# Prologue of a one-core AdaLN, state-space and FFN kernel: POOL's low parts, the modulation and the x projection in another order

## The chip, the cores and the metric

The kernel runs on one core of one Trainium2 chip. The metric is the device time of one execution in microseconds (us); the times of a kernel are the median of its runs. The engines are named as the profile names them: PE (TensorE), DVE (VectorE), ACT (ScalarE), POOL (GpSimd) and SP (SyncE, whose queue issues every DMA of this kernel).

## The reference, cut to what matters

The input u has 4 batches of 512 tokens with 256 channels. A small matrix product of the conditioning c gives six rows of modulation per batch.

```python
mod = (_silu(c) @ wmod).reshape(4, 6, 1, -1)
sa, ca, ga, sb, cb, gb = (mod[:, i] for i in range(6))
...
h = _layernorm(x, axis=-1) * (1 + ca) + sa
x = x + ga * _L0_attn_ref(h, W_in, conv_w, conv_b, z_bias, D, W_out)
h = _layernorm(x, axis=-1) * (1 + cb) + sb
x = x + gb * _L0_ffn_ref(h, W1, W2, W3)
```

In the attention part h is projected by W_in to x (256 channels), B and C (2048 each), z and one a per head (32). x, B and C go through a causal convolution with 4 taps. a goes through a softplus and a running sum over the tokens, and every head's 512 x 512 scores C B^T are weighted by exponents of differences of these sums.

## The kernel before

Everything is float32. A product that must be exact enough is split: each operand has a high part (a cast to the matmul's format) and a low part (the operand minus its high part), and three matmuls hi x hi, hi x lo and lo x hi are added in PSUM.

The order of the work on each engine is written out by hand, as a list of calls in one block per engine, and semaphores tie the engines together. The program has a **prologue** (batch norms, projection and convolution of x, a's running sums), then a long loop over 8 groups of heads times 4 batches (`step`), then the FFN. The change touches the prologue alone. Its chain for a batch b is:

- DVE: `statistics1(b)` (mean and variance of 4 tiles of 128 tokens), POOL: `inverse_root` (1/sqrt of 4 variances for each partition), DVE: `normalise1(b)` (4 instructions that write xn, semaphore `xn_done`).
- PE: `norm_transposes(b)` turns xn into channel rows in PSUM. DVE's `modulation(0)` copies shift and 1 + scale out of PSUM (`mod_ev`); ACT's `h_full(b, kt)` applies them (h32), for both halves kt of the channels. ACT's `h_high` casts h32 to `ht_hi`; POOL's `h_low` subtracts to `ht_lo`.
- PE: `x_project(b, xt)` multiplies by the split weights wx (6 matmuls for each half xt); `a_project(b0)` multiplies h32 of two batches by wa. `warm(n)` issues n matmuls on zeros whose result nobody reads.
- ACT: `x_tap(b, xt)` is the first tap of x's convolution, DVE: `x_tap(b, xt, k)` the three others, each over 512 tokens. With 4 batches and 2 halves DVE has 24 of them.
- a: ACT takes abs, exp and ln, DVE adds (`sp_a`, L1167) and scans over the tokens (L1171, `sums_done`). SP then stores these sums, loads them back broadcast (8 DMAs of `load_sum`), and issues, behind them in its queue, the exchange of x's halves (`swap_halves`) and the stores of x of the batches 2 and 3 (`store_x`). ACT's `last_tap(0, 1, 1)` overwrites the buffer that these stores read and waits for them; `x_evacuate(2, 1)` is queued behind it, and PE's `x_transposes(3, 1)` waits for that.

POOL also splits the weights of x (wx), of the first group of heads (four tiles, `split_tile`) and of z (wz).

The lines that follow are of the kernel before.

Of the kernel before, what the change touches and what calls it, by code (L numbers as in the profile page):

```python
# [19 lines left out]
B, L, D = 4, 512, 256  # L20
# [3 lines left out]
KT = D // P  # L24
CH = L // P
# [3 lines left out]
GT = 4  # L29
# [23 lines left out]
def adaln_ssm_ffn_kernel(nc, u, w_bc, w_x, w_a, w_z, conv, d_rows, z_bias, w_out, w13, w2, c_t, wmod,  # L53
                         consts, out, e_d, gates_d):
    with ExitStack() as ctx:
# [6 lines left out]
        ps = ctx.enter_context(nc.psum_tensor("ps", [P, 8, BANK], F32))  # L62
# [80 lines left out]
        xt = sb("xt", [P, KT, L], F32)  # L143
# [235 lines left out]
        def _(pe):  # L379
# [22 lines left out]
            def norm_transposes(b):  # L402

                pe.wait_ge(s["xn_done"], CH * (b + 1))
                if b >= 2:
                    pe.wait_ge(s["h32_done"], KT * (2 * b - 3))
                for c in range(CH):
                    for kt in range(KT):
                        i = nc.tensor.transpose(ps[:, (4 if b == 1 else 2) + kt, c * P:(c + 1) * P],
                                                xn[:, b % 2, c, kt * P:(kt + 1) * P], ident)  # L410
                i.then_inc(s["lnT_mm"], 1)
# [11 lines left out]
            def x_project(b, xt):  # L423

                pe.wait_ge(s["hlo_done"], KT * (b + 1))
                if b >= 2:
                    pe.wait_ge(s[f"xtaps{xt}"], 3 * (b - 1))
                for kt in range(KT):
                    i = split_mm(ps[:, GT * (b % 2) + xt, :], wx_hi[:, xt, kt, :], wx_lo[:, xt, kt, :],
                                 ht_hi[:, kt, b * L:(b + 1) * L], ht_lo[:, kt, b * L:(b + 1) * L],  # L430
                                 kt == 0, kt == KT - 1)
                i.then_inc(s["xp_mm"], 1)

            def a_project(b0):

                pe.wait_ge(s["h32_done"], KT * (b0 + 2))
                for kt in range(KT):
                    for b in (b0, b0 + 1):
                        i = mm(ps[b * NH:(b + 1) * NH, 6, :], wa_sb[:, kt, :], h32[:, b % 2, kt, :],
                               start=(kt == 0), stop=(kt == KT - 1), skip_group_check=True)  # L440
                        if kt == KT - 1:
                            i.then_inc(s["a_mm"], 1)
# [35 lines left out]
            def warm(n):  # L478

                for k in range(n):  # L480
                    mm(ps[:, 1, :], zeros[:, 0:P], zeros[:], start=True, stop=True)  # L481
# [20 lines left out]
            modulation((0, 1), 0)  # L502
            pe.wait_ge(s["ld_ident"], 16)
            norm_transposes(0)
            norm_transposes(1)
            warm(10)
            pe.wait_ge(s["ld_wa"], 16)
            a_project(0)
            norm_transposes(2)
            pe.wait_ge(s["mod_ev"], 2)  # L510
            pe.wait_ge(s["wx_split"], 2)
            x_project(0, 0)
            x_project(0, 1)
            norm_transposes(3)
            x_project(1, 0)
            x_project(1, 1)
            a_project(2)
            x_project(2, 0)
            pe.wait_ge(s["ld_wmod2"], 16)
# [260 lines left out]
        def _(act):  # L780
# [5 lines left out]
            def h_full(b, kt):  # L786

                n = KT * b + kt
                act.wait_ge(s["lnT_mm"], b + 1)
                if b >= 2:  # L790
                    act.wait_ge(s["hlo_done"], n - 3)
                    act.wait_ge(s["a_mm"], 2)
                af(h32[:, b % 2, kt, :], ps[:, (4 if b == 1 else 2) + kt, :], ACT.Identity, bias=shift[:, 0, kt, b:b + 1],
                   scale=scale1[:, 0, kt, b:b + 1]).then_inc(s["h32_done"], 1)

            def h_high(b, kt):

                act.wait_ge(s["h32_done"], KT * b + kt + 1)
                nc.scalar.copy(ht_hi[:, kt, b * L:(b + 1) * L], h32[:, b % 2, kt, :]).then_inc(s["hhi_done"], 1)

            def x_tap(b, xt):

                n = 2 * b + xt
                act.wait_ge(s["xp_mm"], n + 1)
                w = conv_sb[:, NG * GT + xt, :]
                af(acc[:, n // GT, n % GT, :], ps[:, GT * (b % 2) + xt, :], ACT.Identity, bias=w[:, TAPS:TAPS + 1],
                   scale=w[:, TAPS - 1:TAPS]).then_inc(s["xtap"], 1)
# [7 lines left out]

            act.wait_ge(s["mod_ev"], 2)
            h_full(0, 0)
            h_full(0, 1)
            h_full(1, 0)
            h_high(0, 0)  # L820
            h_full(1, 1)
            h_high(0, 1)
            h_high(1, 0)
            h_high(1, 1)
            h_full(2, 0)
            h_high(2, 0)
            h_full(2, 1)
            act.wait_ge(s["ld_conv"], 16)
            x_tap(0, 0)
            h_high(2, 1)  # L830
            x_tap(0, 1)
            h_full(3, 0)
            h_full(3, 1)
            x_tap(1, 0)
# [234 lines left out]
        def _(dve):  # L1069
# [40 lines left out]
            def normalise1(b):  # L1110
                if b >= 2:
                    dve.wait_ge(s["lnT_mm"], b - 1)
                normalise(u_sb[:, b * CH:(b + 1) * CH, :], xn[:, b % 2], b, norm1_names)
# [12 lines left out]
            def modulation(n):  # L1126

                dve.wait_ge(s["mod_mm"], 4 * (n + 1))
                mod = ps[:, 7 * n, 0:2 * KT * B].rearrange("p (k m b) -> p k m b", k=2, m=KT)
                nc.vector.tensor_copy(shift[:, n], mod[:, 0]).then_inc(s["mod_ev"], 1)  # L1130
                ts(scale1[:, n], mod[:, 1], 1.0, None, ALU.add).then_inc(s["mod_ev"], 1)
# [10 lines left out]
            statistics1(0)  # L1142
            statistics1(1)
            normalise1(0)
            normalise1(1)
            modulation(0)
            statistics1(2)
            statistics1(3)
            normalise1(2)
# [247 lines left out]
        def _(pool):  # L1397
# [37 lines left out]
            def inverse_root(n, eps_name, name):  # L1435

                await_unit(eps_name, n + 1)
                gp.tensor_tensor(rstd[:, n % 2], vareps[:, n % 2], minus_half[:], ALU.pow).then_inc(s[name], 1)  # L1438

            def h_low(b, kt):  # L1440

                pool.wait_ge(s["hhi_done"], KT * b + kt + 1)
                gp.tensor_tensor(ht_lo[:, kt, b * L:(b + 1) * L], h32[:, b % 2, kt, :],
                                 ht_hi[:, kt, b * L:(b + 1) * L].bitcast(F32), ALU.subtract).then_inc(s["hlo_done"], 1)
# [4 lines left out]
            gp.tensor_copy(wx_hi[:], wx_raw[:]).then_inc(s["wx_split"], 1)  # L1449
            pool.wait_ge(s["wx_split"], 1)  # L1450
            gp.tensor_tensor(wx_lo[:], wx_raw[:], wx_hi[:].bitcast(F32), ALU.subtract).then_inc(s["wx_split"], 1)
            inverse_root(2, "eps1", "rs")
            inverse_root(3, "eps1", "rs")
            h_low(0, 0)
            h_low(0, 1)
            h_low(1, 0)
            h_low(1, 1)
            h_low(2, 0)
            pool.wait_ge(s["ld_wg"], 16)
            split_tile(0, 1)  # L1460
            h_low(2, 1)
            split_tile(0, 0)
            h_low(3, 0)
            split_tile(0, 3)
            split_tile(0, 2)
            h_low(3, 1)
            pool.wait_ge(s["ld_wz"], 16)
            gp.tensor_copy(wz_hi[:], wz_raw[:]).then_inc(s["wz_split"], 1)
            pool.wait_ge(s["wz_split"], 1)
# [220 lines left out]
```

## Time and profile before

| what | value |
|---|---|
| median of 3 runs | 534.34 us (533.17 to 534.63) |
| profiled execution, its own time | 538.0 us |
| its span in the profile | 535.8 us |
| mean granted clock of PE | 0.987 |
| PE busy | 520.5 us, 97% |
| DVE busy | 451.6 us, 84% |
| ACT busy | 367.1 us, 69% |
| POOL busy | 240.0 us, 45% |

The span is what the profile's times count from; 2.2 us of the profiled execution's own time lie around it. A busy share is an average over the program; the prologue is its first 60 us. In a timeline a row is a run of like instructions: start, time from the first one's start to the last one's end, engine, line, operation, output and inputs, their number, and in brackets the idle time of the engine before it with what ended it. Neighbours on one engine overlap by some 0.1 us in these rows, so a start to the next start is the better measure of what an instruction costs in a row.

### The profile page before, as it was taken

The page shows a single profiled execution, that of the slowest core. Times are in us where ns is not written, and L with a number is a line of the kernel's source. Part 1 is how long each engine was busy: PE and PEld are TensorE (multiplying, and loading weights), DVE is VectorE, ACT ScalarE, POOL GpSimd, SP SyncE. Part 2 cuts the span into 40 slices and gives each one's busy share as a digit, 9 for nine tenths or more (in the row PEclk, how much of TensorE's full clock was granted, in tenths as well). Part 3 has the DMA queues.
Part 4 walks back from the last instruction along what each step waited for, and adds up shares of the span by engine and source line. Part 5 has one row for each costly group of instructions (what it writes and reads, how often), then busy time and mean ns, then how long its engine had stood idle before and what let it go on. Part 6 is the DMA issues. An engine that isn't in the chain of part 4 may idle for free.

```text
span 535.8 us, 19307 instructions
## 1 busy us (share of the span) xinstructions
PE 520.5 (97%) x7188; PEld 429.9 (80%) x7188; DVE 451.6 (84%) x746; ACT 367.1 (69%) x988; POOL 240.0 (45%) x465
## 2 busy tenths in 40 slices
PE   6998999999999999999999999998999999999997
PEld 3666788888888888888888888876889889889886
DVE  6899699999999999999999999998666656656342
ACT  1777789899898998988899899887424224234240
POOL 6763237777776766776786474581000000000000
PEclk9899899999999999999999999999999999999999
DMA  7736153343333335332432535576430232100101
GB/s 248 299 111 214 49 144 102 98 130 112 109 108 102 125 100 180 128 102 84 142 93 84 152 89 163 146 219 193 125 95 25 80 81 77 40 0 2 40 0 40
DMA packets 50289, 59.40 MB, mean 111 GB/s; under 512 B 8004, under 2 KB 44740, under 8 KB 49864
## 3 DMA queue, kind: packets, MB, share of 16 engines
q1 hardware_dynamic: 50248, 58.88, 35.9%
q8 instruction: 22, 0.36, 0.3%
q14 instruction: 19, 0.16, 0.1%
HBM read 48.75 MB, written 9.05 MB: 108 GB/s over the span
## 4 chain that ended last, share of the span: by engine, by line
PE 87%; DVE 4%; DMA 4%; SPq 2%; issue 1%; POOL 1%; ACT 1%; DVEq 0%; ACTq 0%; POOLq 0%
PE ps L384 20%; PE ps L385 20%; PE ps L386 20%; PE ps L574 9%; PE ps L548 5%; PE ps L629 4%; PE ps L595 3%; PE ps L612 3%; PE ps L698 2%; DVE acc L1123 2%; DMA gates<-gate_rows 2%; DMA x_channels<-acc 1%; SPq L247 1%; PE ps L481 1%; DMA u_sb<-in_u 1%
## 5 line engine op out<-in xcount | busy, mean ns | idle before, releaser
L1212 DVE SCALAR_TENSOR_TENSOR acc<-ps,cw_dve,acc 128x511 f32<-128x511 f32 (+2 forms) x384 | 255.9, 738 | 6.2 <-ACT acc L863 5.9
L1512 POOL TENSOR_TENSOR sums<-sums,far_above 128x256 f32<-128x256 f32 x128 | 94.5, 742 | 112.5 <-DMA sums<-packed_sums 106.4
L898 ACT ACTIVATE decay<-sums,p_slot 128x128 f32<-128x128 f32 (+1 forms) x512 | 143.2, 363 | 1.2 <-ACT p_slot L975 0.7
L863 ACT ACTIVATE acc<-ps,cw_act 128x512 f32<-128x512 f32 x128 | 95.4, 769 | 18.7 <-PE ps L386 16.6
L384 PE MATMUL ps<-ht_hi,wg_hi 128*128 128x512 f32 x256 | 107.5, 420 | 0.1
L385 PE MATMUL ps<-ht_lo,wg_hi 128*128 128x512 f32 x256 | 101.9, 398 | 0.0
L386 PE MATMUL ps<-ht_hi,wg_lo 128*128 128x512 f32 x256 | 101.9, 398 | 0.0
L1039 ACT ACTIVATE silu_sb<-ps 128x512 f32<-128x512 f32 x32 | 19.2, 599 | 78.6 <-PE ps L386 78.6
L1438 POOL TENSOR_TENSOR rstd<-vareps,minus_half 128x4 f32<-128x4 f32 x8 | 8.4, 1047 | 121.9 <-DVE vareps L1093 119.6
L386 PEld LDWEIGHTS ps<-ht_hi,wg_lo 128*128 128x128 f32 x256 | 48.5, 189 | 11.6
L1350 DVE TENSOR_TENSOR hid<-ps,silu_sb 128x512 f32<-128x512 f32 x32 | 22.1, 691 | 42.0 <-ACT silu_sb L1039 41.8
L384 PEld LDWEIGHTS ps<-ht_hi,wg_hi 128*128 128x128 f32 x256 | 48.6, 190 | 9.7 <-issue 0.6
L385 PEld LDWEIGHTS ps<-ht_lo,wg_hi 128*128 128x128 f32 x256 | 49.0, 191 | 8.9
L574 PE MATMUL ps<-acc 64*64 64x64 f32 (+1 forms) x2048 | 52.3, 250 | 0.1
L384 PE MATMUL ps<-h_hi,w_hi 128*128 128x512 f32 x128 | 50.5, 394 | 0.0
L574 PEld LDWEIGHTS ps<-acc 64*64 64x64 f32 x2048 | 47.6, 133 | 3.1
L386 PE MATMUL ps<-h_hi,w_lo 128*128 128x512 f32 x128 | 49.9, 390 | 0.0
L385 PE MATMUL ps<-h_lo,w_hi 128*128 128x512 f32 x128 | 49.9, 390 | 0.0
L887 ACT COPY b_tok<-ps 128x384 f32<-128x384 f32 x64 | 30.4, 474 | 14.5 <-PE ps L548 14.1
L1199 DVE TENSOR_TENSOR mix<-ps,decay 128x1024 f32<-128x1024 f32 x32 | 38.8, 1213 | 0.0
L384 PE MATMUL ps<-w_hi,hid_hi 128*128 128x256 f32 x128 | 37.0, 289 | 0.2 <-DVE stage L1366 0.2
L385 PE MATMUL ps<-w_lo,hid_hi 128*128 128x256 f32 x128 | 36.2, 283 | 0.0
(144 smaller groups left out, 917.6 us busy)
## 6 DMA issues: line engine op xcount, KB each, us to landing
sums<-packed_sums SPq DMA_DIRECT2D x256, 96.0 KB, 2.7
wg_raw<-in_w_bc SPq DMA_DIRECT2D x8, 512.0 KB
y_parts<-yt_sb SPq DMA_DIRECT2D x64, 64.0 KB, 2.1
stage<-y_parts SPq DMA_DIRECT2D x32, 128.0 KB, 2.9
u_sb<-in_u SPq DMA_DIRECT2D x4, 512.0 KB, 4.9
stage<-in_w SPq DMA_DIRECT2D x1, 2048.0 KB, 14.0
x_channels<-acc SPq DMA_DIRECT2D x8, 256.0 KB, 2.5
ee<-running_sums SPq DMA_DIRECT2D x8, 256.0 KB, 3.9
```

Source lines behind the costliest of these rows:

```text
L384: mm(o, w_hi, x_hi, start=first, stop=False)
L385: mm(o, w_hi, x_lo, start=False, stop=False)
L386: return mm(o, w_lo, x_hi, start=False, stop=last)
L548: i = nc.tensor.transpose(ps[:, 6 if p else PROJ_BANK[0], c * P:(c + 1) * P], acc[:, b % 2, p, c * P:(c + 1) * P], ident)
L574: i = mm(ps[NS * at:NS * (at + 1), SCORE_BANKS[bank], o:o + P - NS * h], acc[own, b % 2, p, c * P + NS * h:c * P + NS * (h + 1)], acc[own, ...
L863: af(acc[:, b % 2, t, :], ps[:, PROJ_BANK[t], :], ACT.Identity, bias=cw_act[:, t, 1:2], scale=cw_act[:, t, 0:1]).then_inc(s[f"tap_a{t}"], 1)
L887: nc.scalar.copy(b_tok[:, p, :], ps[:, 6 if p else PROJ_BANK[0], 0:3 * P]).then_inc(s["bt_ev"], 1)
L898: i = af(decay_f[:, m:m + P - NS * h], sums[:, j, own], ACT.Exp, scale=-1.0, bias=p_slot[:, b * CH + n, j:j + 1])
L1199: tt(mix_f[:, 0:2 * BANK].rearrange("p (a l) -> p a l", a=2), ps[:, 2:4, :], decay_f[:, 0:2 * BANK].rearrange("p (a l) -> p a l", a=2), AL ...
L1212: stt(a[:, d:], ps[:, PROJ_BANK[t], 0:L - d], cw_dve[:, t, TAPS - 1 - d:TAPS - d], a[:, d:], ALU.mult, ALU.add).then_inc(s[f"taps{t}"], 1)
L1350: tt(hid[:, m % 2, :], ps[:, 2 + m % 2, :], silu_sb[:, m % 2, :], ALU.mult).then_inc(s["hid_done"], 1)
L1512: gp.tensor_tensor(v, v, far, ALU.add).then_inc(s["masked"], 1)
```

## The change

It does five things, all in the prologue.

1. POOL computes the low parts of batch 0 ahead of the inverse roots of the batches 2 and 3, then waits until DVE has written all norms (`xn_done` at 16), then computes the other six low parts, and only then splits the four weight tiles, which stood between them.
2. DVE's `modulation(0)` stands between the norms of batch 0 and of batch 1.
3. PE has 5 warming matmuls in place of 10, ahead of the transposes of batch 1.
4. PE projects x of the batches 0 and 1 in two parts: the 8 matmuls on the high part of h, for which the low part isn't needed, then the 4 on its low part. Batch 0 stands ahead of `a_project(0)`; batch 1's transposes of batch 3 stand between its parts.
5. ACT casts batch 0 as soon as each half is there, and does batch 0's two taps ahead of batch 2.

```diff
+            def x_project_high(b):
+                pe.wait_ge(s["hhi_done"], KT * (b + 1))
+                for xt in range(2):
+                    for kt in range(KT):
+                        o, x = ps[:, GT * (b % 2) + xt, :], ht_hi[:, kt, b * L:(b + 1) * L]
+                        mm(o, wx_hi[:, xt, kt, :], x, start=(kt == 0), stop=False, skip_group_check=True)
+                        mm(o, wx_lo[:, xt, kt, :], x, start=False, stop=False, skip_group_check=True)
+            def x_project_low(b):
+                pe.wait_ge(s["hlo_done"], KT * (b + 1))
+                for xt in range(2):
+                    for kt in range(KT):
+                        i = mm(ps[:, GT * (b % 2) + xt, :], wx_hi[:, xt, kt, :], ht_lo[:, kt, b * L:(b + 1) * L],
+                               start=False, stop=(kt == KT - 1), skip_group_check=True)
+                    i.then_inc(s["xp_mm"], 1)
...
             norm_transposes(0)
+            pe.wait_ge(s["mod_ev"], 2)
+            warm(5)
             norm_transposes(1)
-            warm(10)
+            pe.wait_ge(s["wx_split"], 2)
+            x_project_high(0)
+            x_project_low(0)
             pe.wait_ge(s["ld_wa"], 16)
             a_project(0)
             norm_transposes(2)
-            pe.wait_ge(s["mod_ev"], 2)
-            pe.wait_ge(s["wx_split"], 2)
-            x_project(0, 0)
-            x_project(0, 1)
+            x_project_high(1)
             norm_transposes(3)
-            x_project(1, 0)
-            x_project(1, 1)
+            x_project_low(1)
             a_project(2)
...
             act.wait_ge(s["mod_ev"], 2)
             h_full(0, 0)
+            h_high(0, 0)
             h_full(0, 1)
+            h_high(0, 1)
             h_full(1, 0)
-            h_high(0, 0)
             h_full(1, 1)
-            h_high(0, 1)
             h_high(1, 0)
             h_high(1, 1)
-            h_full(2, 0)
-            h_high(2, 0)
-            h_full(2, 1)
             act.wait_ge(s["ld_conv"], 16)
             x_tap(0, 0)
+            x_tap(0, 1)
+            h_full(2, 0)
+            h_full(2, 1)
+            h_high(2, 0)
             h_high(2, 1)
-            x_tap(0, 1)
             h_full(3, 0)
...
             normalise1(0)
+            modulation(0)
             normalise1(1)
-            modulation(0)
...
+            h_low(0, 0)
+            h_low(0, 1)
             inverse_root(2, "eps1", "rs")
             inverse_root(3, "eps1", "rs")
-            h_low(0, 0)
-            h_low(0, 1)
+            pool.wait_ge(s["xn_done"], CH * B)
             h_low(1, 0)
             h_low(1, 1)
             h_low(2, 0)
+            h_low(2, 1)
+            h_low(3, 0)
+            h_low(3, 1)
             pool.wait_ge(s["ld_wg"], 16)
             split_tile(0, 1)
-            h_low(2, 1)
             split_tile(0, 0)
-            h_low(3, 0)
             split_tile(0, 3)
             split_tile(0, 2)
-            h_low(3, 1)
```

On PE, at the start of the program, the order of before is this (L481 is `warm`, L397 the modulation's product, L409 a batch's 8 transposes as one or two batches in a row, L439 `a_project`, L384 to L386 one split product of x):

```order
L481 MATMUL ps<-sums 128x512 x20
L397 MATMUL ps<-c_silu,wmod_sb 32x4 x32
L409 MATMUL ps<-cst,xn 128x128 x16
L481 MATMUL ps<-sums 128x512 x10
L439 MATMUL ps<-h,wa_sb 32x512 x4
L409 MATMUL ps<-cst,xn 128x128 x8
L384 MATMUL ps<-ht_hi,wx_hi 128x512
L385 MATMUL ps<-ht_lo,wx_hi 128x512
L386 MATMUL ps<-ht_hi,wx_lo 128x512
```

The same stretch of the changed kernel (L499 is `warm`, L440 and L441 the high part's matmuls, of which three more pairs follow ahead of L448, the low part's; L457 is `a_project`):

```order
L499 MATMUL ps<-sums 128x512 x20
L397 MATMUL ps<-c_silu,wmod_sb 32x4 x32
L409 MATMUL ps<-cst,xn 128x128 x8
L499 MATMUL ps<-sums 128x512 x5
L409 MATMUL ps<-cst,xn 128x128 x8
L440 MATMUL ps<-ht_hi,wx_hi 128x512
L441 MATMUL ps<-ht_hi,wx_lo 128x512
...
L448 MATMUL ps<-ht_lo,wx_hi 128x512 x4
L457 MATMUL ps<-h,wa_sb 32x512 x4
L409 MATMUL ps<-cst,xn 128x128 x8
```

So x of batch 0 has moved ahead of `a_project(0)` and of batch 2's transposes, and half of the warming matmuls are gone.

On POOL, in the middle of the prologue, the order of before is this (rstd is an inverse root, ht_lo a low part of h, wg the split of a weight tile, wz that of z's weights):

```order
L1451 TENSOR_TENSOR wx_lo<-wx_raw,wx_hi 128x512
L1438 TENSOR_TENSOR rstd<-vareps,minus_half 128x4 x2
L1443 TENSOR_TENSOR ht_lo<-h,ht_hi 128x512 x5
L1431 CAST wg_hi<-wg_raw 128x256
L1433 TENSOR_TENSOR wg_lo<-wg_raw,wg_hi 128x256
L1443 TENSOR_TENSOR ht_lo<-h,ht_hi 128x512
L1431 CAST wg_hi<-wg_raw 128x256
L1433 TENSOR_TENSOR wg_lo<-wg_raw,wg_hi 128x256
L1443 TENSOR_TENSOR ht_lo<-h,ht_hi 128x512
```

The same stretch of the changed kernel:

```order
L1469 TENSOR_TENSOR wx_lo<-wx_raw,wx_hi 128x512
L1461 TENSOR_TENSOR ht_lo<-h,ht_hi 128x512 x2
L1456 TENSOR_TENSOR rstd<-vareps,minus_half 128x4 x2
L1461 TENSOR_TENSOR ht_lo<-h,ht_hi 128x512 x6
L1449 CAST wg_hi<-wg_raw 128x256
L1451 TENSOR_TENSOR wg_lo<-wg_raw,wg_hi 128x256
L1449 CAST wg_hi<-wg_raw 128x256
L1451 TENSOR_TENSOR wg_lo<-wg_raw,wg_hi 128x256
```

Two low parts have moved ahead of the last two inverse roots; the six others stand together behind them, and behind the wait for the norms; all four weight splits follow. SP's order is the same in both kernels.

## Rows read from the trace of the kernel before

**Rows 1.** The page: the span, and each engine's busy time.

```profile
span 535.8 us, 19307 instructions
PE 520.5 (97%) x7188; PEld 429.9 (80%) x7188; DVE 451.6 (84%) x746; ACT 367.1 (69%) x988; POOL 240.0 (45%) x465
```

**Rows 2.** Windows of PE: length, busy (count), granted clock, DMA share, GB/s.

```profile
15.00:16.00 1.00, 1.00 (x4) 0.50 1.00 406
...
57.00:58.00 1.00, 1.00 (x4) 0.50 0.00 0
```

**Rows 3.** The chain of work that ended last, from 30 to 56 us.

```profile
35.45 1.14 DVE sums_t L1171
...
47.90 5.28 DMA x_channels<-acc
```

**Rows 4.** Timeline of DVE in the prologue.

```profile
13.09 1.39 DVE L1087 BATCH_NORM_STATS2 stats<-u_sb 128x6 f32<-128x256 f32 x4
...
16.83 1.38 DVE L1100 TENSOR_SCALAR xn<-u_sb,meanvar,rstd 128x256 f32<-128x256 f32 x4
18.36 5.02 DVE L1100 TENSOR_SCALAR xn<-u_sb,meanvar,rstd 128x256 f32<-128x256 f32 x4 [0.15 <-POOL rstd L1438]
24.72 0.75 DVE L1123 SCALAR_TENSOR_TENSOR acc<-ps,conv_sb,acc 128x511 f32<-128x511 f32 x1 [1.34 <-ACT acc L806]
25.83 8.88 DVE L1123 SCALAR_TENSOR_TENSOR acc<-ps,conv_sb,acc 128x511 f32<-128x511 f32 x13 [0.36 <-ACT acc L806]
...
35.37 1.21 DVE L1171 TENSOR_TENSOR_SCAN sums_t<-reset,sp_a 128x512 f32<-128x512 f32 x1
```

**Rows 5.** Timeline of POOL in the prologue.

```profile
11.29 1.26 POOL L1451 TENSOR_TENSOR wx_lo<-wx_raw,wx_hi 128x512 fp32r<-128x512 f32 x1
...
17.09 1.16 POOL L1438 TENSOR_TENSOR rstd<-vareps,minus_half 128x4 f32<-128x4 f32 x1 [0.89 <-DVE vareps L1093]
18.08 6.54 POOL L1443 TENSOR_TENSOR ht_lo<-h,ht_hi 128x512 fp32r<-128x512 f32 x5
...
25.14 0.73 POOL L1433 TENSOR_TENSOR wg_lo<-wg_raw,wg_hi 128x256 fp32r<-128x256 f32 x1 [0.18 <-POOL wg_hi L1431]
...
35.37 2.28 POOL L1470 TENSOR_TENSOR wz_lo<-wz_raw,wz_hi 128x512 fp32r<-128x512 f32 x1
```

**Rows 6.** Timeline of ACT in the prologue.

```profile
13.20 1.45 ACT L793 ACTIVATE h<-ps,shift,scale 128x512 f32<-128x512 f32 x2 [10.62 <-DVE scale L1131]
...
16.94 1.65 ACT L799 CAST ht_hi<-h 128x512 fp32r<-128x512 f32 x3
...
25.68 1.45 ACT L793 ACTIVATE h<-ps,shift,scale 128x512 f32<-128x512 f32 x2
...
29.00 1.12 ACT L799 CAST ht_hi<-h 128x512 fp32r<-128x512 f32 x2
...
33.85 0.63 ACT L844 ACTIVATE a_work<-a_work 128x512 f32<-128x512 f32 x1
```

**Rows 7.** Timeline of PE in the prologue.

```profile
10.39 1.06 PE L409 MATMUL ps<-cst,xn 128*128 128x128 f32 x8 [1.20 <-DVE xn L1100]
13.07 1.97 PE L409 MATMUL ps<-cst,xn 128*128 128x128 f32 x8 [1.62 <-DVE xn L1100]
...
18.85 1.91 PE L439 MATMUL ps<-h,wa_sb 128*32 128x512 f32 x8
...
21.54 0.48 PE L384 MATMUL ps<-ht_hi,wx_hi 128*128 128x512 f32 x1
...
24.43 1.04 PE L409 MATMUL ps<-cst,xn 128*128 128x128 f32 x8
...
28.21 1.91 PE L439 MATMUL ps<-h,wa_sb 128*32 128x512 f32 x8
...
54.65 0.63 PE L453 MATMUL ps<-cst,acc 128*128 128x128 f32 x4 [2.29 <-ACT x_tok L813]
...
56.62 0.63 PE L384 MATMUL ps<-ht_hi,wg_hi 128*128 128x512 f32 x1
```

## The prediction, made before the changed kernel ran

> **What bounds the kernel now.** I read the page first: PE is busy for 520.5 of 535.8 us [rows 1], so what happens in the prologue counts only through the moment at which PE can leave it. The reader should therefore look for what PE waits for in the first 55 us. PE's timeline shows it: idle for 2.29 us until 54.65, ended by ACT's copy of x [rows 7]. The chain of waits, followed back from there, says what that copy stood behind [rows 3]: a convolution tap that waited for the stores of x, issued until 47.90 and landed 5.28 later; these came after a row of SP's issues; and the first of those waited for a's running sums, whose scan starts on DVE at 35.45 in the chain and ends at 36.59. From the scan's end to 54.65 are 18.1 us in which SP issues DMAs back to back and waits for transfers. The change touches none of it. So the question is how much earlier the scan ends.
>
> Ahead of the scan DVE is the tight engine. It does 13 taps without a gap from 25.83 to 34.7, then a's sum and the scan [rows 4]: 8.88/13 gives 0.68 a tap where they follow each other. Ahead of that it loses time. The four norms of batch 2 took 1.38 us, the like four of batch 3 took 5.02 [rows 4], in a stretch where POOL did low parts of h, 5 in 6.54 us [rows 5]; then DVE stood 1.34 and 0.36 for taps from ACT [rows 4].
>
> **What the change costs and gives, step by step.** I carry the times of before through the new orders.
>
> *Start.* PE transposes batch 0 at 10.39 to 11.45 [rows 7]. ACT started only at 13.20, since the modulation's copy on DVE stood behind both norms [rows 6]; now the modulation is there by 10.6 (batch 0's norms are done at 10.39 [rows 7], and two copies of 8 columns follow), and ACT starts at 11.5. An h takes 0.78 and the next follows after 0.67; casts in a row follow after 0.51 and take 0.62 [rows 6]. With a cast behind its own h, ACT has both halves of batch 0 cast at 11.5 + 2 x (0.78 + 0.62) less a 0.1 of overlap, 14.2. POOL's two low parts (6.54/5, 1.3 each [rows 5]) end at 15.5; before, they ended at 18.08 + 2.6, 20.7.
>
> *PE to its next fixed point.* The modulation wait costs nothing (10.6 against 11.45). The 5 warming matmuls run at 11.45; those of before took (18.85 - 15.04)/10, 0.4 each, since PE's granted clock was 0.50, its lower level of 1.2 GHz [rows 2, 7]. So they end at 13.3. The transposes of batch 1 take 1.97 at that level and end near 15.2 [rows 7]; x's weights are split by 12.55 [rows 5]. A matmul of x at 2.4 GHz costs (24.43 - 21.54)/12, 0.24 [rows 7]. Then high part 8 x 0.24 to 17.1; low part 4 x 0.24 to 18.05 (its input is there at 15.5); `a_project(0)` 1.85 to 19.9; transposes of batch 2 to 20.95; high part of batch 1 to 22.85; transposes of batch 3 to 23.9; low part to 24.85. The transposes of batch 3 also need ACT to have emptied the banks of batch 2: 20.95 + 1.5, in time.
>
> *The norms.* Statistics of the batches 2 and 3 take 13.09 to 16.83 as before [rows 4]. The inverse roots (1.1 each [rows 5]) stand behind the low parts, 15.5, and are there at 16.6 and 17.7. The first is still ahead of the end of the statistics, 16.8, so batch 2's norms come as before, by 18.2; a root beside them does not hold them (1.38 with the root at 17.09 beside them [rows 4, 5]). Batch 3's take 1.4 instead of 5.0 because POOL stands still: done by 19.3, 4 us earlier. PE wants them at 22.85. POOL then does batch 1's low parts 19.3 to 21.9, and PE wants them at 23.9: 2 us of slack, which is the price of POOL's wait, fully covered. Whether statistics are themselves held by a low part no row shows. Bounds: nothing, or, held as the norms were, up to two low parts, 2.6 us, which pushes the last norm to 21.9 at most and batch 1's low parts to 24.5; then PE stands 0.6. I take nothing, as the low end of 0 to 0.6.
>
> *ACT and DVE after it.* ACT does batch 3's two h from 23.9 to 25.4 and the taps of batch 1 at 25.25, so DVE's sixth tap can start at 26.0. Before it started at 25.83 + 4 x 0.68, 28.5 [rows 4]. `a_project(2)` starts at 25.4, 2.8 earlier than 28.21 [rows 7]. DVE is no longer late for itself here: it has done its first five taps by 19.3 + 5 x 0.68, 22.7, and waits 3.3. From the sixth tap on DVE, PE and ACT keep their order. ACT's last casts go from 29.00 to 26.5, and with it the end of the ln from 34.48 to about 32.0 [rows 6]; DVE, which wanted it 0.7 ahead of the scan at 35.37, wants it at 34.7 - 2.6, 32.1. So the three engines move together by 2.5 to 2.8. I take 2.6.
>
> *The scan.* POOL's weight splits, which stood between low parts, come later: the last low part starts after ACT's casts and ends at 29.8, and the four subtractions of 0.73 [rows 5] fall, one every 1.3 us, between 30.3 and 34.8. The scan falls between 32.7 and 33.9, so it meets one. Before it met the split of z: the subtraction took 2.28, where the same shape took 1.26 [rows 5], and the scan its full speed of 1.21 [rows 4]. So it was POOL that waited there, 1.0. Here it can be either: if it is the scan, that costs up to the 0.7 of a subtraction, if it is POOL, nothing. I take 0.2, nearer to the row, in which the scan ran and POOL waited. The Trainium skill has this as a rule (SBUF — State Buffer, Who interferes with whom): a VectorE instruction with two SBUF inputs and a GpSimd instruction that reads SBUF exclude each other, and whichever starts first holds the port for its whole length. By that rule, the trace of before agrees (2.28 against 1.26), and a subtraction that starts ahead of the scan would charge up to 0.7, which gives 1.9 and 532.4. The weight tiles are wanted by PE at 37.4, so their delay costs nothing.
>
> *Behind the scan* the 18.1 us stay, as SP's order is the same and the loads at the start have long landed. PE arrives at its wait 2.4 earlier too, so the idle 2.29 remains, and the stretch at the lower level that follows it, with matmuls 0.43 apart instead of 0.24 [rows 2, 7] (the row at 56.62 is one of eight), remains.
>
> Sum: 2.6 - 0.2 = **2.4 us less**. The profiled execution would go from 538.0 (span 535.8) to 535.6 (span 533.4). The median of the runs shown is 3.7 lower than that execution; the same step from 534.34 gives **531.9 us**, 0.45% faster.
>
> **Rivals.**
>
> *The clock stays low a stretch longer.* PE has less to do ahead of x now, 5 warming matmuls less. Before, it stood idle from 11.45 to 13.07, was at the lower level at 15 to 16 and back at the higher by 18.85 [rows 2, 7]. If it stays low from 15.2 to about 18.6, x of batch 0 costs 0.43 a matmul, 1.5 us more, all of it on PE's way to 24.85. Then 0.9 us less than before, 533.4. For it: nothing shows what PE needs to be raised. Against: in the new order PE works without a gap from 10.39 on. I give 0.17.
>
> *The clock comes back sooner or the second fall is missed.* The first saves 0.9 on batch 1's transposes, the second eight matmuls by 0.19, 1.5. Then 3.3 to 3.9 less: 530.4 to 531.0. Chance 0.12.
>
> *The gain is lost on the way to 54.65.* The stores of x landed in 5.28 us beside other transfers; if they collide otherwise, or the scan waits its 0.7 and ACT's ln is later than I add up, 0.3 to 1.2 us are left: 533.1 to 534.0. Chance 0.14. Against: every transfer there is issued in the same order at the same distance.
>
> *It ends on the other side.* The place is PE from 15.2 on; the mechanism is again the lower level, as long as in the first stretch of before, which lasted from the idle at 11.45 to at most 18.85, 7 us. A low stretch of 7 us from 15.2 costs 7 x (1 - 0.24/0.43), 3.1 us, 0.7 more than the gain: 535.0. It decides from 5.4 us of lower level on; 9 us would be slower by 1.6. For it: x_project's high part would then be the first dense work. Against: before, ten dense matmuls at the lower level were enough to end it. Chance 0.07.
>
> That the edit does not do what it says (DVE's norms still held because POOL's inverse roots hold them) has the rows against it that I gave: 1.38 beside a root.
>
> **How the numbers follow.** The forecast itself, 1.8 to 2.9 less, has 0.50. The likeliest time is 531.9, its own range 531.4 to 532.6. A change below 0.3%, 1.6 us, cannot be told from none here. Faster by more: 0.50 + 0.12, and 0.03 of the third rival's upper end, 0.65. Within: 0.29. Slower by more: 0.06, most of the fourth. For 8 in 10 the range takes in the missed fall of the clock (530.4) and the first and third rival down to 534.0; it leaves out the slower one.
>
> **What would show it.** Right: norms of batch 3 in 1.4 us; ACT's first h near 11.5; DVE's first tap before 20 with a new idle of about 3 us behind the fifth; the scan's end at 34 to 34.4; PE's idle ending near 52.2. Wrong: a granted clock of 0.50 beyond 16 us, the scan stretched to 1.9, low parts of batch 1 that PE waits for, or an idle ahead of 52 us that grew by as much as the prologue gained.

## The result and the profile after

The changed kernel took 531.25 us in the median of 7 runs (529.46 to 531.95), the kernel before 534.63 us in 7 runs beside them (533.17 to 536.10). The ratio is 0.9921 with a 95% interval of 0.9894 to 0.9949, so 0.8% faster, 3.4 us where 2.4 were forecast. Run again later, it gave 531.20 us in 12 runs (529.94 to 534.25), ratio 0.9951, interval 0.9928 to 0.9974. Over all the runs whose clock is listed, which the 7 of the kernel before above are not, the medians are 534.37 us (94 runs of the kernel before) and 531.21 us (19 of the changed one), 3.2 us apart. The first set's 531.25 us lies just below the prediction's own range (531.4 to 532.6) and inside its range for 8 in 10 (530.4 to 534.0).

The two profiled spans differ by far more, 535.8 [rows 1] against 527.6:

```profile
span 527.6 us, 19297 instructions
PE 513.4 (97%) x7182; PEld 425.6 (81%) x7183; DVE 446.5 (85%) x746; ACT 367.2 (70%) x988; POOL 239.8 (45%) x465
```

That is one execution of each, and part of the 8.2 us is chance. At the end of PE's wait near 50 us the two are 5.3 us apart: 3.8 at the scan's end and 1.5 more behind it. The other 2.9 come later, where PE's granted clock fell to 0.50 twice more in the kernel before (56 to 59 us and 374 to 376 us) and not once in this execution of the changed kernel. First DVE's timeline of the changed kernel, which answers to [rows 4]:

```profile
12.49 1.41 DVE L1105 BATCH_NORM_STATS2 stats<-u_sb 128x6 f32<-128x256 f32 x4 [1.14 <-DMA u_sb<-in_u]
...
16.74 2.68 DVE L1118 TENSOR_SCALAR xn<-u_sb,meanvar,rstd 128x256 f32<-128x256 f32 x8 [0.16 <-POOL rstd L1456]
19.33 3.63 DVE L1141 SCALAR_TENSOR_TENSOR acc<-ps,conv_sb,acc 128x511 f32<-128x511 f32 x5
24.94 6.00 DVE L1141 SCALAR_TENSOR_TENSOR acc<-ps,conv_sb,acc 128x511 f32<-128x511 f32 x9 [1.99 <-ACT acc L824]
...
31.60 1.22 DVE L1189 TENSOR_TENSOR_SCAN sums_t<-reset,sp_a 128x512 f32<-128x512 f32 x1
```

The norms of the batches 2 and 3 are one run of 8 in 2.68 us, where the last four alone had taken 5.02. The first tap starts at 19.33 instead of 24.72. Then the new idle, 1.99 us ahead of the sixth tap, and the scan's row starts at 31.60 instead of 35.37.

POOL's timeline, which answers to [rows 5]:

```profile
13.14 2.52 POOL L1461 TENSOR_TENSOR ht_lo<-h,ht_hi 128x512 fp32r<-128x512 f32 x2
15.62 2.22 POOL L1456 TENSOR_TENSOR rstd<-vareps,minus_half 128x4 f32<-128x4 f32 x2
19.50 5.11 POOL L1461 TENSOR_TENSOR ht_lo<-h,ht_hi 128x512 fp32r<-128x512 f32 x4 [1.66 <-DVE xn L1118]
26.16 2.55 POOL L1461 TENSOR_TENSOR ht_lo<-h,ht_hi 128x512 fp32r<-128x512 f32 x2 [1.55 <-ACT ht_hi L817]
...
31.76 1.59 POOL L1451 TENSOR_TENSOR wg_lo<-wg_raw,wg_hi 128x256 fp32r<-128x256 f32 x1 [0.18 <-POOL wg_hi L1449]
```

POOL stands still for 1.66 us until the norms are done, and the subtraction of the third weight split, which starts 0.16 us after the scan, waits for it: 1.59 us where it takes 0.73 alone [rows 5].

ACT and PE, which answer to [rows 6, 7]:

```profile
11.21 0.78 ACT L811 ACTIVATE h<-ps,shift,scale 128x512 f32<-128x512 f32 x1 [8.47 <-PE ps L409]
```

```profile
12.02 1.04 PE L409 MATMUL ps<-cst,xn 128*128 128x128 f32 x8
14.12 0.47 PE L440 MATMUL ps<-ht_hi,wx_hi 128*128 128x512 f32 x1 [1.05 <-ACT ht_hi L817]
...
16.06 1.09 PE L448 MATMUL ps<-ht_lo,wx_hi 128*128 128x512 f32 x4
17.08 1.91 PE L457 MATMUL ps<-h,wa_sb 128*32 128x512 f32 x8
...
24.29 1.91 PE L457 MATMUL ps<-h,wa_sb 128*32 128x512 f32 x8 [0.60 <-ACT h L811]
...
32.96 1.09 PE L482 MATMUL ps<-cst,sums_t 128*64 128x128 f32 x16 [0.71 <-DVE sums_t L1189]
...
49.33 0.63 PE L471 MATMUL ps<-cst,acc 128*128 128x128 f32 x4 [0.75 <-ACT x_tok L831]
```

The transposes of batch 1 take 1.04 here, not 1.97, because PE's clock did not fall. Windows of PE (length, busy, granted clock, DMA) show it, in answer to [rows 2]:

```profile
12.00:13.00 1.00, 1.00 (x9) 1.00 0.97 352
...
15.00:16.00 1.00, 1.00 (x6) 1.00 1.02 414
```

PE's wait that ended at 54.65 now ends at 49.33, and is 0.75 us instead of 2.29. The row at 32.96 matters below: PE itself waits for the scan, whose sums it transposes.

### The profile page after: what moved, and what is told of

It reads as the page before. It is cut to its first block, busy times and chain, and to the rows that moved or that the text cites. A ratio compares the mean times of both kernels' runs of the same rounds, so it can differ in the third digit from the quotient of the medians.

```text
span 527.6 us, 19297 instructions
## 1 busy us (share of the span) xinstructions
PE 513.4 (97%) x7182; PEld 425.6 (81%) x7183; DVE 446.5 (85%) x746; ACT 367.2 (70%) x988; POOL 239.8 (45%) x465
## 4 chain that ended last, share of the span: by engine, by line
PE 82%; DVE 10%; ACT 2%; DMA 2%; issue 2%; POOL 1%; SPq 0%; DVEq 0%; POOLq 0%; ACTq 0%
PE ps L384 19%; PE ps L385 18%; PE ps L386 18%; PE ps L592 8%; DVE acc L1230 5%; PE ps L566 4%; PE ps L647 4%; PE ps L613 3%; PE ps L630 2%; PE ps L716 2%; DMA gates<-gate_rows 1%; DVE mix L1217 1%; DVE acc L1141 1%; DMA u_sb<-in_u 1%; DVE mix L1219 1%
## 5 line engine op out<-in xcount | busy, mean ns | idle before, releaser
L384 PE MATMUL ps<-ht_hi,wg_hi 128*128 128x512 f32 x256 | 107.0, 418 | 0.0
L386 PE MATMUL ps<-ht_hi,wg_lo 128*128 128x512 f32 x256 | 101.2, 396 | 0.0
L386 PEld LDWEIGHTS ps<-ht_hi,wg_lo 128*128 128x128 f32 x256 | 48.2, 188 | 11.6
L384 PEld LDWEIGHTS ps<-ht_hi,wg_hi 128*128 128x128 f32 x256 | 48.2, 188 | 9.3 <-issue 0.4
L385 PEld LDWEIGHTS ps<-ht_lo,wg_hi 128*128 128x128 f32 x256 | 48.6, 190 | 8.8
L384 PE MATMUL ps<-h_hi,w_hi 128*128 128x512 f32 x128 | 50.5, 394 | 0.0
L386 PE MATMUL ps<-h_hi,w_lo 128*128 128x512 f32 x128 | 49.9, 390 | 0.0
L384 PE MATMUL ps<-w_hi,hid_hi 128*128 128x256 f32 x128 | 37.0, 289 | 0.2 <-DVE stage L1384 0.2
```

The source lines that it names most:

```text
L384: mm(o, w_hi, x_hi, start=first, stop=False)
L385: mm(o, w_hi, x_lo, start=False, stop=False)
L386: return mm(o, w_lo, x_hi, start=False, stop=last)
```

## The experiments

Each was timed against the kernel before on the same chip, and each has one profiled execution. "Like the changed kernel" below means a ratio whose interval overlaps both of the changed kernel's.

### 1. The kernel before, again

> The kernel before, unchanged, to see how its profile and its granted clock differ from one execution to the next. If the 8.2 us between the two profiled spans are all the change, its span is again 535 to 536 with a clock of 0.987 or so. If some of it is chance in PE's clock, its runs spread over several us and the shorter ones have the higher mean clock, by about 1.6 us for each stretch of 3.4 us at the lower level; the chain's step from the scan's end to the end of PE's wait near 54 us stays at about 18.

Measured: 535.68 us (532.01 to 537.92, 10 runs), ratio to its other runs 1.0026 (1.0002 to 1.0050); there is no edit, and the interval still leaves out 1, so a difference of 0.3% is not to be read from such an interval. The profiled span is 532.9. DVE, the chain and PE of this execution:

```profile
24.65 0.75 DVE L1123 SCALAR_TENSOR_TENSOR acc<-ps,conv_sb,acc 128x511 f32<-128x511 f32 x1 [1.75 <-ACT acc L806]
...
35.30 1.21 DVE L1171 TENSOR_TENSOR_SCAN sums_t<-reset,sp_a 128x512 f32<-128x512 f32 x1
```

```profile
47.83 3.89 DMA x_channels<-acc
```

```profile
53.20 0.63 PE L453 MATMUL ps<-cst,acc 128*128 128x128 f32 x4 [0.92 <-ACT x_tok L813]
```

The prologue is the same to 0.07 us up to the scan. Behind it the stores of x land in 3.89 us, not 5.28 [rows 3], and PE's wait ends 1.45 earlier; no fall of the clock follows it. So from the scan's end to the end of that wait are 16.7 us here (35.38 + 1.14, in the chain, to 53.20), not the 18.1 on which the prediction built. That expectation missed. What differed in the transfer is not shown.

The runs also show the clock's part. Each run has a mean granted clock, and the medians go with it:

| mean clock of the run | kernel before | changed kernel |
|---|---|---|
| 1.000 | 532.79 us (2 runs) | 530.12 us (6 runs) |
| 0.997 | 533.16 us (27) | 531.81 us (5) |
| 0.994 | 533.88 us (14) | 531.78 us (4) |
| 0.990 | 535.00 us (41) | none |
| 0.987 | 537.65 us (4) | none |

(Values of the clock between these have one or two runs each and are left out.) At the same mean clock the two are 1.4 to 2.7 us apart. The rest of the 3.2 goes with the clock, whose mean over the runs is 0.9928 before and 0.9968 after. The table shows that time and clock go together, not which fall costs what. The profiles show where the falls are: both of the kernel before have the granted clock at 0.50 from 12 to 18 us and again near 372 us, after PE has waited 2.3 to 2.5 us for a norm. Both of the changed kernel stay up at either place, though PE waited 2.08 and 2.65 us there. Experiments 2 and 8 (0.997) fell only at the second place, which the change does not touch. No path shown here leads from the change to the second place, so that share of the gap may be chance.

### 2. The change without POOL's standing still

```diff
-            pool.wait_ge(s["xn_done"], CH * B)
```

> The changed kernel without POOL's wait for the norms; everything else as changed. Theory A (POOL's standing still frees DVE's norms, but DVE waits for ACT's tap after its fifth tap anyway): the norms of batch 3 go from 1.4 to about 3 to 4 us beside low parts of batch 1, DVE's idle of 2.0 us before the sixth tap shrinks by as much, and the time stays within 0.5 us. Theory B (the wait carries the gain): about 2 us slower than the changed kernel. Theory C (POOL's wait costs more than it gives, since the low parts of batch 1 come 2 us earlier without it): up to 0.3 us faster.

Measured: 531.21 us (12 runs), ratio 0.9950 (0.9930 to 0.9971), like the changed kernel. DVE and POOL:

```profile
19.01 3.08 DVE L1118 TENSOR_SCALAR xn<-u_sb,meanvar,rstd 128x256 f32<-128x256 f32 x4 [0.15 <-POOL rstd L1456]
22.02 9.52 DVE L1141 SCALAR_TENSOR_TENSOR acc<-ps,conv_sb,acc 128x511 f32<-128x511 f32 x14
```

```profile
18.73 2.56 POOL L1461 TENSOR_TENSOR ht_lo<-h,ht_hi 128x512 fp32r<-128x512 f32 x2
```

The norms of batch 3 are held again, 3.08 us instead of 1.38, and DVE has no idle of note among the 14 taps that follow. Most of the 1.7 us come out of the idle that DVE had anyway; the scan's row starts at 32.20, 0.6 later than in the changed kernel's profile. Theory A fits: POOL's wait for the norms is worth nothing that these runs can tell.

### 3. The change with 10 warming matmuls

```diff
-            warm(5)
+            warm(10)
```

> The changed kernel with 10 warming matmuls in place of 5. Theory A (the gain is PE's shorter way through the prologue): at the higher level of the clock five more cost about 1.1 us on PE, of which 1.05 are idle before x's high part now, so 0 to 0.3 us slower; at the lower level 2.1 us, so about 1 us slower. Theory B (PE's clock is what counts, and more dense work keeps it up): a higher mean clock over the runs and 0.5 us or more faster.

Measured: 531.66 us (7 runs), ratio 0.9948 (0.9930 to 0.9967), like the changed kernel, with a mean clock of 0.997 over its runs as well. In its profiled execution, the slowest of the seven, the matmuls ran at the lower level, and the sixth tap came at 26.85 instead of 24.94:

```profile
11.98 3.39 PE L499 MATMUL ps<-sums 128*128 128x512 bf16 x9 [0.22 <-issue]
15.21 1.04 PE L409 MATMUL ps<-cst,xn 128*128 128x128 f32 x8
```

The mean clock is no higher than the changed kernel's, so theory B falls; what the five matmuls cost is within the interval.

### 4. The change with a later scan

```diff
+            for k in range(3):
+                nc.vector.memset(xn2[:], 0.0).then_inc(s["pad"], 1)
+                dve.wait_ge(s["pad"], k + 1)
             dve.wait_ge(s["aln_done"], 1)
```

> The changed kernel with three fills of 1024 columns of an idle buffer on DVE just ahead of the sum of a, which make the scan later by their length (1.5 to 3 us by the row). Theory A (the scan's end sets the end, one to one, through SP's row of issues): the kernel is slower by 0.8 to 1.0 of the scan's delay. Theory B (behind the scan something else decides, as the landing of the stores of x or PE's own work): slower by less than half of the delay.

Measured: 537.21 us (6 runs), ratio 1.0060 (1.0040 to 1.0080). DVE and PE:

```profile
32.19 0.91 DVE L1185 MEMSET xn<- 128x1024 f32 x1 [0.16 <-issue]
...
36.27 1.52 DVE L1192 TENSOR_TENSOR_SCAN sums_t<-reset,sp_a 128x512 f32<-128x512 f32 x1
```

```profile
37.94 1.85 PE L482 MATMUL ps<-cst,sums_t 128*64 128x128 f32 x16 [4.60 <-DVE sums_t L1192]
```

The fills delay the sum of a by 3.6 us (three, each 1.19 after the last), and the median is 6.0 above the changed kernel's 531.21. So the scan's end does set the end, but at more than one to one, which neither theory had. The delay becomes idle time of PE, 4.60 us, and PE works at the lower level after it: the transposes behind it take 1.85, not 1.09, and from the scan's end to the end of PE's wait are 18.1 us, where the changed kernel has 16.5. With the scan, which took 1.52 instead of 1.22, that makes 5.5 of the 6.0.

### 5. POOL's new order alone

On the kernel before, the hunk of POOL from the change, nothing else.

> The kernel before with POOL's new order alone (batch 0's low parts ahead of the last two inverse roots, the wait for the norms, splits last). In the kernel before ACT casts batch 0 only by 17.6 us, so the roots wait behind low parts that end near 19. Theory A (the parts of the change need each other): the norms of batch 3 take 1.4 us but end near 22.6 instead of 23.4, DVE's first tap is not earlier than 24, and the time is within 1 us of before, rather slower. Theory B (POOL's wait alone carries the gain, by freeing DVE's norms of 3.6 us): 2 us or more faster than before.

Measured: 536.23 us (12 runs, one of them 571.0, which the ratio leaves out), ratio 1.0022 (0.9997 to 1.0047): no gain. Theory A fits, B falls. DVE and POOL:

```profile
19.77 2.67 DVE L1100 TENSOR_SCALAR xn<-u_sb,meanvar,rstd 128x256 f32<-128x256 f32 x8 [2.28 <-POOL rstd L1438]
25.24 0.75 DVE L1123 SCALAR_TENSOR_TENSOR acc<-ps,conv_sb,acc 128x511 f32<-128x511 f32 x1 [2.79 <-ACT acc L806]
...
35.89 1.70 DVE L1171 TENSOR_TENSOR_SCAN sums_t<-reset,sp_a 128x512 f32<-128x512 f32 x1
```

```profile
16.20 2.49 POOL L1443 TENSOR_TENSOR ht_lo<-h,ht_hi 128x512 fp32r<-128x512 f32 x2 [4.22 <-ACT ht_hi L799]
```

The norms are freed, and come later: their roots stand behind low parts for which POOL waited 4.22 us, as ACT starts late without the earlier modulation. DVE is done with the norms at 22.4, and then waits 2.79 for the tap.

### 6. Everything but POOL

On the changed kernel, POOL's order of before.

> The changed kernel with POOL's order of before: everything but POOL. Theory A (low parts of batch 0 come behind both roots, from 17.6 on, so PE holds at x's low part of batch 0 until about 20.2 where the changed kernel had it at 16.1): DVE's sixth tap at 28 to 29, scan's end near 36, the time within 1 us of before. Theory B (PE's and ACT's new order with fewer warming matmuls carries the gain): as fast as the changed kernel within 0.7 us.

Measured: 537.82 us (12 runs), ratio 1.0061 (1.0038 to 1.0084), 3.3 us slower than before. PE:

```profile
20.43 1.20 PE L448 MATMUL ps<-ht_lo,wx_hi 128*128 128x512 f32 x4 [3.40 <-POOL ht_lo L1461]
21.56 3.59 PE L457 MATMUL ps<-h,wa_sb 128*32 128x512 f32 x8
```

PE has nothing left ahead of x's low part and waits 3.40 us for POOL; the work behind it runs at the lower level, 3.59 for 1.91. Theory A has the place right and the size too small: the sixth tap comes at 31.11, not at 28 to 29, and the time is not within 1 us of before. Theory B falls.

### 7. The kernel before with 5 warming matmuls

```diff
-            warm(10)
+            warm(5)
```

> The kernel before with 5 warming matmuls in place of 10, nothing else. Theory A (in the kernel before PE reached x of batch 0 at 21.5 where its low part was there at 20.7, so PE's warming was late by at most 0.9 us): 0.5 to 1.0 us faster than before, scan's end 0.8 earlier. Theory B (warming matmuls are the gain): 2 us or more faster. Theory C (less dense work keeps the clock low for longer): slower, with a lower mean clock over its runs.

Measured: 533.27 us (12 runs), ratio 0.9982 (0.9960 to 1.0005). The scan's row starts at 34.87, 0.5 earlier:

```profile
34.87 1.22 DVE L1171 TENSOR_TENSOR_SCAN sums_t<-reset,sp_a 128x512 f32<-128x512 f32 x1
```

Theory A fits, but a ratio of 1 is inside the interval. B and C fall.

### 8. The ln first

```diff
-            x_tap(2, 0)
             act.wait_ge(s["aexp_done"], 1)
             af(a_exp, a_exp, ACT.Ln, bias=1.0).then_inc(s["aln_done"], 1)
+            x_tap(2, 0)
```

and on DVE the taps (2, 0, 0) and (2, 0, 1) behind the scan.

> The changed kernel with ACT's ln (and its table load) ahead of the first tap of batch 2, and DVE's sum and scan of a two taps earlier. The scan's end should come about 1.1 us earlier. Theory A (the scan's end sets the end): about 1 us faster than the changed kernel. Theory B (with the scan at 32.8 PE's own work is as late, as its idle near 49 us is only 0.75): at most 0.7 us faster, the idle near 49 us gone.

Measured: 530.73 us (6 runs), ratio 0.9920 (0.9888 to 0.9952), like the changed kernel. The scan's row starts at 30.38 instead of 31.60. PE no longer waits for the scan, but waits at 36.04 for a tap of DVE that now stands behind the scan; its wait near 49 us ends only 0.55 earlier and is as long as in the changed kernel:

```profile
30.38 1.22 DVE L1187 TENSOR_TENSOR_SCAN sums_t<-reset,sp_a 128x512 f32<-128x512 f32 x1
```

```profile
36.04 0.50 PE L384 MATMUL ps<-ht_hi,wg_hi 128*128 128x512 f32 x1 [0.85 <-DVE acc L1141]
...
48.78 0.63 PE L471 MATMUL ps<-cst,acc 128*128 128x128 f32 x4 [0.75 <-ACT x_tok L831]
```

So 0.7 of 1.2 us are lost behind the scan. B's size fits, but the idle that it wanted gone stayed.

### 9. The kernel before, 5 warming matmuls between the transposes

```diff
+            warm(5)
             norm_transposes(1)
-            warm(10)
```

> The kernel before with 5 warming matmuls, and these between the transposes of batch 0 and batch 1, where the changed kernel has them. The run with 5 in the old place had its lower level of the clock once in the prologue, the kernel before in both its profiles twice in a row. Theory A (the place of the matmuls sets the clock, and the clock alone is not the gain): the lower level lasts at most 3.5 us in the prologue, the scan's end is near 36 as with 5 in the old place, 0.7 to 1.3 us faster than before. Theory B (a clock that stays up is most of the gain): 2 us or more faster than before.

Measured: 534.00 us (12 runs), ratio 0.9988 (0.9968 to 1.0009). The scan's row starts at 34.78, as in experiment 7. The transposes of batch 1 took 1.09, so the clock was up there; it fell later, for `a_project(0)`, 3.05 us instead of 1.91, behind an idle of 2.48:

```profile
16.63 3.05 PE L439 MATMUL ps<-h,wa_sb 128*32 128x512 f32 x8 [2.48 <-ACT h L793]
```

Theory A fits, though a ratio of 1 is inside the interval, and B falls. A clock that is up for the transposes brings nothing that the interval tells to the kernel before, which then waits for ACT's h of batch 1.

### 10. The changed kernel, again

> The changed kernel, unchanged, for its spread and a second profile. If the first profile owed about 1 us to the clock, which stayed up throughout, the runs have scan ends between 32.8 and 34 and spans between 527.6 and 530.5, and most have at least one stretch at the lower level; the median is 530.5 to 531.5.

Measured: as given at the top, 531.20 us. The median is as expected, and 9 of the 12 runs have a mean clock below 1.000; their spans reach 532.4, further than the 530.5 expected. Its profile has a span of 528.5 and again no fall of the clock in the prologue. DVE, and the low parts of POOL beside it:

```profile
14.49 1.25 DVE L1111 TENSOR_SCALAR vareps<-meanvar 128x4 f32<-128x4 f32 x1
...
25.02 6.00 DVE L1141 SCALAR_TENSOR_TENSOR acc<-ps,conv_sb,acc 128x511 f32<-128x511 f32 x9 [1.01 <-ACT acc L824]
...
31.67 1.22 DVE L1189 TENSOR_TENSOR_SCAN sums_t<-reset,sp_a 128x512 f32<-128x512 f32 x1
```

```profile
13.18 2.54 POOL L1461 TENSOR_TENSOR ht_lo<-h,ht_hi 128x512 fp32r<-128x512 f32 x2
```

One thing differs ahead of the sixth tap. The small instruction that adds epsilon to the variances (`vareps`) took 1.25 us where it takes 0.17: it ended with POOL's second low part, which had started at 14.40. In the changed kernel's first profile it ran at 14.26, just ahead of that low part. Here the last norm is done at 20.5, not 19.4, and PE stood 0.30 for batch 1's low part; DVE's idle ahead of the sixth tap took up the rest.

### 11. x of the batches 0 and 1 whole

```diff
-            x_project_high(0)
-            x_project_low(0)
+            x_project(0, 0)
+            x_project(0, 1)
...
-            x_project_high(1)
             norm_transposes(3)
-            x_project_low(1)
+            x_project(1, 0)
+            x_project(1, 1)
```

> The changed kernel with x of the batches 0 and 1 projected whole, three matmuls at a time, which waits for the low parts from the start. In the changed kernel x's high part ran from 14.1 to 16.1 and the low part was there at 15.7. Theory A (high parts first are worth what PE would stand): PE starts x of batch 0 at 15.7 instead of 14.1, 1.5 us later, which passes to the sixth tap and the scan: 1.0 to 1.5 us slower than the changed kernel. Theory B (at the lower level of the clock PE comes at 15.2 anyway): 0.3 to 0.7 us slower.

Measured: 534.31 us (12 runs), ratio 1.0002 (0.9976 to 1.0027): the whole gain is gone. PE:

```profile
16.30 0.47 PE L384 MATMUL ps<-ht_hi,wx_hi 128*128 128x512 f32 x1 [0.81 <-POOL ht_lo L1461]
...
19.26 1.91 PE L457 MATMUL ps<-h,wa_sb 128*32 128x512 f32 x8
21.11 1.09 PE L409 MATMUL ps<-cst,xn 128*128 128x128 f32 x8
23.83 1.07 PE L409 MATMUL ps<-cst,xn 128*128 128x128 f32 x8 [1.63 <-ACT h L811]
...
27.62 1.91 PE L457 MATMUL ps<-h,wa_sb 128*32 128x512 f32 x8
```

Both expectations were too small, since they counted one place of two. The first: PE stands 0.81 for the low part with the high part still to do, and `a_project(0)` starts 2.2 later than at 17.08. Half of that is the clock and the start: experiment 4's profile, whose clock also fell there, has it at 18.16, 1.1 earlier than here. The second: the transposes of batch 3 need the banks that ACT empties of batch 2, and with no high part of batch 1 between the two transposes PE stands 1.63; `a_project(2)` starts 2.2 later than in experiment 4 (27.62 against 25.37). Then the scan met a weight split and, unlike above, was itself held:

```profile
34.70 1.78 DVE L1189 TENSOR_TENSOR_SCAN sums_t<-reset,sp_a 128x512 f32<-128x512 f32 x1
```

### 12. The ln first and ACT's copy ahead of the tap

Experiment 8 and, on ACT:

```diff
             x_evacuate(2, 0)
-            last_tap(0, 1, 1)
             x_evacuate(2, 1)
+            last_tap(0, 1, 1)
```

> The changed kernel with the ln first, as above, and ACT's copy of x that PE waits for near 49 us ahead of the tap that waits for the stores of x. Theory A (PE's own work is the bound there, the copy its last wait of 0.75, and the wait for the stores of x no longer reaches PE): the idle of 0.75 is gone, and the time is 0.5 to 0.9 us below that of the kernel with the ln first, 530.0. Theory B (what PE does next waits for the tap just as long): no change from that kernel, the idle moved to the next transposes.

Measured: 529.63 us (528.80 to 531.57, 8 runs), ratio 0.9915 (0.9886 to 0.9944), the lowest median of the study, 4.7 us below that of the kernel before. The changed kernel's ratio on the same chip was 0.9951 (0.9928 to 0.9974); the intervals overlap, so that it beats the changed kernel is likely and not shown. PE near 49 us:

```profile
47.75 1.04 PE L471 MATMUL ps<-cst,acc 128*128 128x128 f32 x8
48.62 0.49 PE L566 MATMUL ps<-cst,acc 128*128 128x128 f32 x3
49.51 0.48 PE L384 MATMUL ps<-ht_hi,wg_hi 128*128 128x512 f32 x1 [0.40 <-ACT b_tok L905]
```

The two transposes of batch 3 are one run of 8, the wait of 0.75 is gone, and an idle of 0.40 comes back one step on, for another copy of ACT. Theory A holds for the place, and half of the idle has moved as B said. That copy is still queued behind the tap, but the tap waited only 0.15 us here, for PE, and not for the stores of x.

## Why the prediction was right, point by point

- **The start held.** Forecast: ACT's first h at 11.5, casts by 14.2, low parts by 15.5. Measured: 11.21, 13.97, 15.66.
- **The norms held**, in the first profile: all done at 19.4 (19.3), batch 3's in 1.4 us, POOL's wait covered. Statistics beside low parts were not held (1.41 for four in both cases), but the small instruction behind them can be (1.17 to 1.25 for 0.17 in experiments 2, 3, 8, 10, 11 and 12). I had bounded that at 0 to 0.6 us of PE and taken 0; PE stood 0.30 to 0.33 for it in experiments 10 and 12. Experiment 2 goes further than I did: no effect of POOL's wait shows in the time.
- **PE to 24.85 was mis-sized, by the clock.** I placed the high part at 15.2, with 5 matmuls and the transposes at the lower level. In the profiles of experiments 10 and 12 and of the changed kernel the clock stayed up, the high part started at 14.12 to 14.15, held by ACT's cast, and the sixth tap came near 25.0, not 26.0. In experiment 4, whose edit comes later, the clock fell there and the sixth tap came at 26.02, as forecast. So both cases occur. The first set's 3.4 is in the range of the second rival (clock up, 3.3 to 3.9 less), to which I gave 0.12.
- **The scan**: forecast to end near 34.2, it ended at 32.8: 1.1 us from the clock, 0.2 because POOL waited for it (1.59 against 0.73), which is the 0 of my 0 to 0.7. So the term of 2.6 for DVE, PE and ACT together was 3.7 to 3.8 in the two profiles of the changed kernel, whose clock stayed up. Experiments 5 and 11 show the other end, 0.5 to 0.6.
- **"Behind the scan the 18.1 us stay" failed.** I took SP's issues and the landing in 5.28 for fixed, and the path through the stores of x for the one that counts. The same kernel gave 3.89 and 16.7 in its second profile, the changed kernel 16.5, and ten of the fourteen profiles lie at 16.5 to 16.9. There a second path is as long, which I had not followed: PE waits for the scan itself (0.71 at 32.96) and then has its own matmuls up to 48.6, with one idle of 0.39. ACT's tap ahead of the copy waited for PE in the changed kernel and in experiments 4, 6, 7 and 8 (0.62 to 0.63 us), and for the stores in experiments 1, 2, 3, 5, 9, 10 and 11 (0.63 to 0.91), so the two tie within 0.3 us. The idle of 2.29 and the fall after it, which I carried over into the changed kernel, stand in one profile of the fourteen. That carrying them over did no harm to the forecast was luck: only 4 of the 94 runs of the kernel before have a mean clock as low as that profile's 0.987, and what neither kernel usually has falls out of the difference. The step from the scan's end to the end still passes on the delay (experiment 4), but an earlier scan only in part (experiment 8), since PE then waits for DVE's taps instead.
- **The sum.** 2.4 forecast; 3.4 and 2.6 measured in the two sets, 3.2 over all. At the same mean clock it is 1.4 to 2.7. The term that was missing is the clock: I treated it as a rival that is or isn't, where each execution falls its own number of times, and the changed kernel's fell less often. In the second profiles of both kernels PE's wait ends 3.7 us apart (53.20 and 49.50).
- **What carries the gain** is not one part. POOL's standing still and the number of warming matmuls can be put back without a loss that shows (experiments 2 and 3). POOL's order alone, everything but it, and everything but the high parts have none of the gain (5, 6 and 11). As the rows read, earlier modulation lets ACT start, ACT's order feeds POOL, POOL's order feeds the low part, and the high part fills PE until then and again while ACT empties the banks. No run took out the modulation or ACT's order alone, so their share is argued and not shown. I costed the high part only by its place in PE's sum; without it nothing of the gain was left.

## What to carry to other kernels

When a prologue is a chain over four engines, look for the piece of work that needs the fewest of them and put it where the tight engine would stand; removing one link's delay is worth what the next link's idle leaves of it, which may be nothing. Profile the same kernel twice before a step of its chain is taken as fixed: here a landing moved by 1.4 us, and the median from the highest mean clock to the lowest by 4.9, where the effect is about 3. Follow every path to the wait that is to end earlier, not only the one that ended last. And cost a wait on PE with what follows it: behind idles of 3.40 and 4.60 us (experiments 6 and 4) the matmuls ran at half speed.

## What the hardware showed that I had not expected

- The same stores of x, issued in the same order, landed in 5.28 us in one execution of the kernel before and in 3.89 in another.
- Which of DVE's scan and POOL's subtraction waits is a matter of a tenth of a us, and by these rows it is the one that starts second (at equal starts it was POOL [rows 4, 5]): POOL was stretched from 0.73 to 1.59 in the changed kernel (scan at 31.60, subtraction at 31.76), the scan from 1.21 to 1.70 in experiment 5 (35.89 behind 35.77) and to 1.78 in experiment 11 (34.70 behind 34.67).
- A DVE instruction on 4 columns (`vareps`) can be held as long as a large one: 1.25 us instead of 0.17 in experiment 10, when it started 0.09 us after a low part of 512 columns (14.49 behind 14.40).
- The length of PE's idle alone did not decide whether its clock fell: near 370 us it fell behind an idle of 2.29 in experiment 1 and stayed up behind 2.65 and 2.86 in experiments 10 and 12.
- A POOL instruction with small operands does not hold DVE's norms, a large one does: four norms beside an inverse root took 1.38 us [rows 4, 5], as in experiment 3 the four of batch 3 with POOL standing still, and 5.02 or 3.08 beside low parts.
- Fills that delayed the scan by 3.6 us cost 6.0 us at the end.
